# Three regroupings in an eight-layer transformer on one core: attention A's order, embedded values of R on narrower strips, weighing in W

## The reference

```
x = x + A(norm(x))         # 4 layers: 8 heads of 16; 4 local (window 128), 4 linear causal; MLP 128-512-128
x = x + E(norm(x))         # 8 experts, top 2
x = x + R0(norm(x))        # 16 heads of 8, causal, relative keys and values
x = x + E(norm(x))
x = x + R1(norm(x))        # the same, not causal, distances clipped at 128
x = x + W(norm(x))         # 2 layers: 8 heads of 64, window 64, rotary; gated MLP
x = x + H(norm(x))         # long convolutions by DFT
x = x + W(norm(x))
```

```
att = softmax(q k^T * scale + q . embk[distance])       # (b, h, t, s)
y   = einsum('bhts,bhsd->bhtd', att, v) + einsum('bhts,tsd->bhtd', att, rv)   # rv = embv[distance]
```

## Time and profile before

| | us |
|---|---|
| median of 3 runs | 3053.79 |
| lowest, highest | 3047.31, 3056.62 |
| the profiled execution | 3039.37 |
| its span, first to last instruction | 3037.6 |
| PE busy | 2790.9 (92%) |
| DVE busy | 1947.6 (64%) |
| ACT busy | 1885.4 (62%) |
| POOL busy | 1055.3 (35%) |

### The profile page before, as it was taken

One profiled execution on the slowest core, in us unless ns is written; L12 is line 12 of the kernel. 1 busy time (PEld: TensorE's weight loads), 2 busy tenths in 40 slices (PEclk: granted clock), 3 DMA queues, 4 the chain that ended last, 5 costly groups with the idle time before them and its releaser, 6 DMA issues.

```text
span 3037.6 us, 58842 instructions
## 1 busy us (share of the span) xinstructions
PE 2790.9 (92%) x21780; PEld 1904.2 (63%) x21780; DVE 1947.6 (64%) x5625; ACT 1885.4 (62%) x4404; POOL 1055.3 (35%) x876
## 2 busy tenths in 40 slices
PE   8889989978999999789999999898899998998997
PEld 5565647537888886378888888455355464554554
DVE  6454636376777775778888887675476324764774
ACT  6666766514666764167777777586587514875774
POOL 2222223203233230064545453354255112552551
PEclk9999999988999998999999999999999999999999
DMA  1010000000000000200000000310111001110210
GB/s 52 3 38 1 12 9 1 4 8 1 2 2 2 2 2 3 72 2 2 2 2 2 2 2 2 123 47 21 40 49 32 22 1 54 49 32 24 51 39 14
DMA packets 35262, 62.83 MB, mean 21 GB/s; under 512 B 11526, under 2 KB 15654, under 8 KB 33830
## 3 DMA queue, kind: packets, MB, share of 16 engines
q1 hardware_dynamic: 34982, 59.07, 7.0%
HBM read 23.48 MB, written 1.15 MB: 8 GB/s over the span
## 4 chain that ended last, share of the span: by engine, by line
PE 72%; DVE 10%; ACT 7%; issue 4%; POOL 3%; SPq 2%; DMA 1%; DVEq 0%; POOLq 0%; ACTq 0%
PE bank L779 62%; PE bank L1004 6%; PE bank L1119 3%; SPq L745 2%; POOL work L1903 2%; ACT bank L1245 1%; ACT work L1237 1%; ACT squared L1247 1%; DVE work L1610 1%; ACT work L1269 1%; DVE centered L1481 1%; DVE normed L1488 1%; ACT work L1361 1%; ACT squared L1241 1%; DVE work L1754 1%
## 5 line engine op out<-in xcount | busy, mean ns | idle before, releaser
L1325 ACT ACTIVATE low<-bank,low 128x512 f32<-128x512 f32 (+23 forms) x384 | 227.4, 593 | 331.0 <-DVE low L1667 326.9
L1237 ACT ACTIVATE low<-bank 128x512 f32<-128x512 f32 (+3 forms) x512 | 425.6, 941 | 0.9 <-PE bank L1004 0.9
L779 PE MATMUL bank<-table_keys,halves 128*128 128x512 f32 (+3 forms) x1536 | 419.1, 381 | 0.6 <-ACT low L1325 0.4
L779 PE MATMUL bank<-work 128*64 128x128 f32 (+6 forms) x4480 | 368.2, 291 | 41.0 <-DVE work L1557 16.1
L1667 DVE TENSOR_REDUCE low<-bank 128x1 f32<-128x512 f32 (+22 forms) x512 | 289.5, 572 | 166.1 <-PE bank L779 161.8
L779 PEld LDWEIGHTS bank<-work 128*64 128x64 f32 (+3 forms) x4480 | 266.8, 145 | 192.3 <-issue 143.5
L1857 POOL TENSOR_TENSOR halves<-squared,const 128x512 fp32r<-128x512 f32 x128 | 135.4, 1058 | 578.4 <-PE bank L779 578.4
L1237 ACT ACTIVATE work<-bank 128x512 f32<-128x512 f32 (+4 forms) x389 | 200.8, 539 | 165.1 <-PE bank L779 63.4
L779 PEld LDWEIGHTS bank<-table_keys,halves 128*128 128x128 f32 x1536 | 245.7, 192 | 55.9 <-issue 33.7
L1903 POOL TENSOR_TENSOR work<-work 128x768 f32<-128x768 f32 x128 | 187.7, 1466 | 193.6 <-DVE work L1758 190.5
L1361 ACT ACTIVATE work<-work 128x192 f32<-128x192 f32 (+1 forms) x512 | 218.8, 431 | 49.1 <-DVE work L1747 49.1
(11 more groups left out here) (198 smaller groups left out, 5900.9 us busy)
## 6 DMA issues: line engine op xcount, KB each, us to landing
work<-work SPq DMA_DIRECT2D x512, 64.0 KB, 2.0
slot<-in_wW SPq DMA_DIRECT2D x4, 1605.5 KB, 6.7
slot<-in_wA SPq DMA_DIRECT2D x4, 837.0 KB, 6.1
table_low<-embv_padded SPq DMA_DIRECT2D x2, 1536.0 KB, 6.3
table<-in_dft SPq DMA_DIRECT2D x1, 3072.0 KB, 11.8
slot<-in_wE SPq DMA_DIRECT2D x2, 584.0 KB, 3.9
const<-in_const SPq DMA_DIRECT2D x1, 1094.5 KB, 5.0
squared<-in_x SPq DMA_DIRECT2D x4, 256.0 KB, 6.1
```

Of the source, the lines that this page charges most:

```text
L779: return pe.matmul(o, l, r, start=start, stop=stop)
L1237: return act.activation(dst, src, ACT.Identity)
L1325: act.activation(PR[t.G % 4][:, 0:n], bank[t.G % 2][:, 0:n], ACT.Exp, bias=NBR[:, t.G % 4:t.G % 4 + 1], accum_out=RSR[:, t.G % 8:t.G % 8 + ...
```

## The change

1. **A, order.** In each of the 19 steps, the values of window i-2 move from just after the scores to just ahead of `a_weigh` and `a_turn`, behind context, projection, output projection and norms. To allow it, `QT` and `CN` (queries and context of the linear half) get two buffers. The MLP's step is split in `a_mlp` (up, gelu) and `a_mlp_down`. From the second layer on, `a_project` and `a_linear` of lane 0 move from the layer's start to between up and down of the preceding layer's lane 3.
2. **R, embedded values.** A block's matmul of 64 output rows x 128 columns becomes two of 32 rows x 64 columns: each covers four queries' rows and only the columns of these four (every head's 8 columns are cut in two groups of 4). The rest of the bank, which the mask discards, is set to zero once at the start of each R. The rows used are the same.
3. **W, weighing.** `w_weigh` of pair j moves from the start of step j+1 to step j, behind `w_scale` and ahead of `w_turn`, `w_out`, `shift` and the norms. `shift` gets a wait for all weighings planned ahead of it on POOL itself.

```
-                    if 1 <= j <= len(pairs): ... add("w_weigh", pairs[j - 1])      # at the step's start
+                    if j < len(pairs): ... add("w_weigh", pairs[j])                # behind scale(r - 2)
...
-                        strip = slice(64 * (j % 2), 64 * (j % 2) + 64)
-                        last = mm(o[strip, 0:P], rows_, PT[:, t.slot, max(b, 0), :, t.cols], start=(j < 2), stop=(j + 2 >= len(blocks)))
+                        for part in range(2):
+                            to = 64 * (j % 2) + 32 * part
+                            own = slice(QG // 2 * (1 - part), QG // 2 * (2 - part))
+                            by_head = o[to:to + 32, 0:P].rearrange("p (h q) -> p h q", h=HEADS_R)
+                            last = mm(by_head[:, :, own], rows_[:, 32 * part:32 * part + 32],
+                                      PT[:, t.slot, max(b, 0), :, t.cols][:, :, own],
+                                      start=(j < 2), stop=(j + 2 >= len(blocks)))
...
+                for b in (4, 5):
+                    for to in (0, 64):
+                        mm(bank[b][to:to + 64, 0:P], k_("zeros"), ident)
...
                 add("norm_mean", c=1, **first)
-                add("a_mlp", c=3, load=load)
+                up = add("a_mlp", c=3, load=load)
+                add("a_project", c=0)
+                add("a_linear", c=0)
+                add("a_mlp_down", c=3, load=load, tile=up)
```

More of the change, by code:

```diff
@@ L92, with __init__ @@
 class Step:
-    def __init__(self, kind, n, k, load, stream, norm, updated, shift, affine, rotations, c=0, w=0, i=0, half=0, which=0, conv=0,
+    def __init__(self, kind, n, k, load, stream, norm, updated, shift, affine, rotations, weighed, c=0, w=0, i=0, half=0, which=0, conv=0,
                  x="", pt=0, hp=0, src="", via="", dst="", gain=None, table=None, name="", u=0, tile=None):
@@ L101, in __init__ @@
         self.updated = updated
-        self.affine, self.rotations = affine, rotations
+        self.affine, self.rotations, self.weighed = affine, rotations, weighed
         self.c, self.w, self.i = c, w, i
@@ L130 @@
     "a_out": STREAM,
-    "a_mlp": each("a_gelu", 4) + STREAM,
+    "a_mlp": each("a_gelu", 4),
+    "a_mlp_down": STREAM,
     "gate": (("gate_copied", 1, 1),),
@@ L176, in add @@
                     shift=lane_shift[lane], affine=seen.get("affine", 0),
-                    rotations=seen.get("w_add", 0), **more)
+                    rotations=seen.get("w_add", 0), weighed=seen.get("w_weigh", 0), **more)
         if kind == "norm_scale" and more["gain"]:
@@ L216, in stage_a @@
                 c, w = divmod(i, NT)
-                if i == 0:
+                if i == 0 and layer == 0:
                     add("a_project", c=0)
@@ L246, in stage_a @@
                     add("norm_scale", c=c - 2, **second)
+                if 2 <= i <= C * NT + 1:
+                    if (i - 2) % NT == 0:
+                        held = add("a_values", c=(i - 2) // NT, w=0, i=i - 2)
+                    else:
+                        add("a_values_on", c=(i - 2) // NT, w=(i - 2) % NT, i=i - 2, tile=held)
+                    if (i - 2) % NT == NT - 1:
+                        add("a_heads", c=(i - 2) // NT, tile=held)
                 if i < C * NT:
@@ L345, in stage_w @@
                 r = lane_items + j
-                if 1 <= j <= len(pairs):
-                    lane, i, hp = pairs[j - 1]
-                    add("w_weigh", c=lane, i=i, hp=hp)
                 if lane_items <= r - 1 < C * lane_items:
@@ L368, in stage_w @@
                     scale(r - 2)
+                if j < len(pairs):
+                    lane, i, hp = pairs[j]
+                    add("w_weigh", c=lane, i=i, hp=hp)
                 if c + 1 < C and at in (3, 4, 5, 6):
@@ L507, in carve @@
                 return a
-            names = "abcd"[:len(shape)]
+            names = "abcde"[:len(shape)]
             return a.rearrange(f"p ({' '.join(names)}) -> p {' '.join(names)}",
@@ L891, in a_mlp, with a_mlp_down @@
                     mm(take(s.k + j)[:, :], wt(s, WA, "w1", j * P, P), normed[:, s.c, :]).then_inc(tile_full, 1)
-                o = take(s.k + 4)
+            def a_mlp_down(s):
+                o = take(s.k)
                 for j in range(4):
@@ L1262, in a_context @@
             def a_context(s):
-                copy(QT[0:64, :], full(s.k)[0:64, :]).then_inc(sem("a_q_turned"), 1)
+                copy(QT[0:64, s.c % 2, :], full(s.k)[0:64, :]).then_inc(sem("a_q_turned"), 1)
             def a_scores(s):
```

43 lines of the change are left out of this document (20 added, 23 removed).

## The result

The changed kernel takes **2926.18 us** (median of 4 runs, 2922.62 to 2929.18) against 3055.2 for the kernel before in the same session: a ratio of 0.9582, interval 0.9561 to 0.9603, 4.2% less. The forecast was 2913, with a range from 2877 to 2980. The profiled execution has a span of 2924.8 us.

The account below looks back on a forecast made before the run. PE, busy 92% of the span, was taken to bound the kernel. 80 (R) + 38 (W) + 23 (A) = 141 us off the profiled 3039.4 gave 2898, shifted to 2913 because the runs' median lies 14 us higher; range 2877 to 2980.

Parts of the forecast that it names:

- R, -80: R's embedded values on narrower strips: 87 us less of PE, 7 taken off for DVE, bounds -97 and -40.
- the change of shape: R, embedded values directly ahead of values or fold: no switch of matmul shape, at most 10 us more saved.
- The term for DVE: R's shortest pairs: DVE's own chain of 3.8 us sets the pace there, 7 us taken off the 87.
- W, -38: W's earlier weighing: 38 of the 45.4 us that PE's transposes wait for it go, bounds -46 and -20.
- DVE's new wait is the reciprocal's: W: DVE waits for the pair's exponentials, turned copy and norms queued behind; expected short, except in the last lane.
- A, -23: A's new order: 17 us from waits ahead of the values, 6 at layer boundaries, bounds -10 and -34.
- each layer's end: A: waits of 1.40 and 0.71 us have nothing to cover them, so 4 x 2.1 = 8.4 us stay.
- The boundary: A, start of the next layer: of 4.23 us of PE's waits 2 go, at three boundaries, 6 us.
- DVE's takeover: Rival in R: DVE's chain takes over, R gives 40 us instead of 80, time 2953; chance 0.14.
- Waits that move: Rival in A and W: waits only move one step later, giving 20 us instead of 61, time 2954; chance 0.10.
- Dear pieces of four: Rival in R: groups of four columns cost a round 0.126, R saves 15 us, time 2978; chance 0.08.
- the slower side: Rival in R: strips stop running side by side, 146 us more in R, time 3139; chance 0.04.

Follow-up runs that it names:

- half maxima: Changed kernel, with DVE finding R's maxima over only half of the columns: 2916.32 us, ratio 0.9541; the same edit on the kernel before: 3052.72 us.

## Why the prediction was right, and where it wasn't

**R, -80: measured -70 (61 to 79).** The price of PE was right: 87 us forecast from `fold`'s row, 87 read. That the sum is exact is partly luck. A pair with two blocks was priced at 0.28 everywhere, as if the 0.11 for leaving the narrow shape halved with the rounds; it costs 0.36 ahead of scores and 0.25 ahead of the values. With three blocks 0.56 was forecast, and it is 0.57 and 0.47. The forecast had the change of shape as a term on top, up to 10 us, and left it out of the 80. The term for DVE was 7; in batches at full clock R0 gained 0.95 us in four pairs, one from each batch of a lane (14.63 to 13.68), and R1 1.43 (18.75 to 17.32), so 30.4 + 45.8 = 76: DVE and what else waits took 11 of 87, of which half maxima gave back 6 in the same batches. The step that was mis-sized is this one, by 4 us; its reasoning ("pairs without values or spread are shorter than the mean") is what the short batches show. The remaining 6 lie within the interval. Two things outside the sum are of their size: the larger clearing, some 4 us, and the longer stretch at 1.2 GHz at R0's start (between the table's marks R0 gained 22.5 us, where the batches at full clock give 30.4), the execution profiled before having had its short case. The times can't divide the 6 between them.

**W, -38: measured -34 (23 to 46).** The mechanism was right: 45.4 us of wait became 2.7. The failing step is "DVE's new wait is the reciprocal's": it was seen, with the turned copy behind it, but costed only as "a little". It cost 13 on DVE's copy, and PE's wait for ACT's copies rose as well, from 4.6 to 11.4 us in the two W stages. So 43 us less of one wait and 20 more of two others; the stretch behind R1 became 26 us shorter (medians of the table's column "rest", 1138.6 in the seven rows without W's part and 1112.1 in the five with it as the change has it), a little less than the 34 that the times say. The forecast looked for what is late next in the loop of the weighing; what was late next was the copy behind it, on two engines.

**A, -23: measured -27 (20 to 35).** For the values' move alone 17 was forecast; its time says 25 (15 to 34), the layers of its trace 16 to 18. The total was right; two of its steps weren't, and they cancel (4 x 1.11 and 8 x 0.57 us). One is "each layer's end, 1.40 at 268.74 ..., which has nothing to put there": it became 0.29, while the 0.71 behind it stayed. The other is that a norm's matmul covers the wait: it covers that for the copies, but the second norm's waits itself for its square, eight times 0.57 us. The 1.40 was not a missing filler. DVE's timeline before:

```profile
267.24 0.75 DVE L1488 SCALAR_TENSOR_TENSOR normed<-centered,slot,squared 128x512 f32<-128x512 f32 x1 [3.44 <-ACT squared L1247]
267.91 0.68 DVE L1557 COPY work<-bank 128x512 f32<-128x512 f32 x1
```

The turned copy stood in DVE's queue behind a norm that waited for ACT. In the new order the norm's matmul comes ahead of the transposes, and DVE waits 1.53 us for ACT there instead of 3.44. The boundary was forecast at 6 and measured at 5 (0 to 10), with 3 readable in the trace. The new wait was not one for "the maxima or the weighing" but for the second norm's square, 3.83: DVE's linear part stood ahead of the residual, as the forecast said of the start of the norms; with the linear part moved away 2.94 stayed. "One larger clearing, below 1 us" was right for DVE's own time, 0.85 more, and too small for the layer, 3.8 with the fall of the clock behind it.

**The reference point.** The sum gave 2898 against a profiled execution that lay 14 us below its median, and shifting it to 2913 was right: 128 of the forecast 141 came, and by profiled spans it would have looked like 113: the execution profiled before had neither the fall of the clock at 35 us nor a long stretch at 1.2 GHz at R0's start.

**The rivals.** DVE's takeover happened, at a quarter of its price (some 10 us instead of 40, 7 of them in the sum). Waits that move: W's did by a half of what was won (20 of 43). A's did in part: the wait for the second norm's square grew from 0.2 to 16.2 us, 11.5 of it in place of the 12.7 at the three boundaries. A's time fell by 27 us all the same. Dear pieces of four: refuted, 60 against 59 ns a round. The first wording of the Trainium skill ("Advanced Engine Details and Errata", section PSUM Cachelines: any non-contiguous pattern significantly slows matmuls) doesn't hold for groups of four here. For its second (every two consecutive elements contiguous) the trace has a price where it is broken, 72 against 60 ns. Strips still run side by side: 24 records took 0.57 us, 24 ns each, far from the 52 from which the slower side began. The change did what it says.

## What to carry to other kernels

- Price a narrower matmul by a row of the same shape in the same trace, its way into and out of the shape included: that gave 87 us here, with errors that cancelled. Price the way out of a shape once for each group, not by the round. Then look at the next engine batch by batch; a mean pair with 12% of slack hides batches with none.
- Moving a step ahead means moving its waits ahead. List what stands behind each waiting instruction on every engine it touches; W lost 13 of 43 us to a copy queued behind a reciprocal, and moving that away showed the same wait on ACT.
- A part that is measured alone carries what it drags along. Here every part had the second buffers' clearing, 3.8 us in the first layer.
- A wait ahead of a matmul can be a queue order two engines away. Ask what the releasing engine did before it, before you call for a filler.

## What was unexpected of the hardware

- The stretch at 1.2 GHz at R0's start lasted 24, 34, 41 or 44 us in different executions, for the same code of R too (24 and 44), and is worth up to 9 us. In A's first layer the level fell at 34 to 36 us in ten of the fourteen profiles and not in the others. Four pairs of profiles with the same code there (139.2 and 141.6, 143.0 and 145.4, 130.8 and 133.2, 125.9 and 128.3) put its price at 2.4 us. So a part's gain is better read from batches and periods at the same clock than from spans.
- A matmul whose columns are read and written in groups of four costs a round of 60 ns, contiguous ones 59, single elements at a stride of two 72 (each round four strips of 32 output partitions, 64 columns).
- The step from 32-row strips to the full-width scores shows a price of 0.11 us: the same 16 records take 0.36 us ahead of scores and 0.25 ahead of the values, with 128 columns 0.57 and 0.46.
